# DLRM tower with a compressed interaction network: the first layer's sums over d made by ScalarE's evictions

## The reference

```python
e = stack([tbl_f[ids[:, f]] for f in range(32)], axis=1)      # (2048, 32, 16): b, m, d
x0 = xk = e
outs = []
for W in (W0, W1, W2):                                        # (m, h, k), k = 64; h = 32, 64, 64
    xk = relu(einsum('bmd,bhd,mhk->bkd', x0, xk, W))
    outs.append(sum(xk, axis=2))                              # over d
z = concatenate(outs, axis=1)                                 # (2048, 192)
h = concatenate([z, dense_ctx], axis=1)
h = maximum(h @ W_top1 + b_top1, 0)                           # 512
h = maximum(h @ W_top2 + b_top2, 0)                           # 256
y = h @ W_top3
```

## Time and profile before

| | |
|---|---|
| median of 3 runs | 1216.67 us (1216.64 to 1218.73) |
| the profiled execution's own time | 1227.56 us |
| its span in the profile | 1225.8 us |
| TensorE (PE) matmul busy | 1122.7 us, 92% |
| VectorE (DVE) busy | 1116.5 us, 91% |
| ScalarE (ACT) busy | 731.8 us, 60% |
| GpSimd (POOL) busy | 923.2 us, 75% |
| mean granted clock of TensorE | 0.986 of full speed |

### The profile page before, as it was taken

The page is one execution under the profiler, slowest core; times in us unless marked ns, Lnnn a source line. Parts: engine busy times, 40 slices in busy tenths (PEclk is TensorE's granted clock), DMA queues, the critical chain, the costliest instruction groups (busy, mean ns, idle before and its releaser), DMA issues.

```text
span 1225.8 us, 14619 instructions
## 1 busy us (share of the span) xinstructions
PE 1122.7 (92%) x5312; PEld 395.7 (32%) x5312; DVE 1116.5 (91%) x519; ACT 731.8 (60%) x1361; POOL 923.2 (75%) x642
## 2 busy tenths in 40 slices
PE   0267999999999999999999999999999999999997
PEld 0022233333343333334333333333333333333334
DVE  0158999999999999999999999999999999999994
ACT  0036656765675666666666766576576657657652
POOL 6767888788887878788787878878787887875400
PEclk9878999999999999999999999999999999999998
DMA  5967877657688676768877566787767677776200
GB/s 117 188 126 157 166 152 148 140 120 150 133 167 166 137 147 125 146 128 159 167 149 148 119 144 131 151 165 152 152 130 141 130 146 158 164 153 131 53 1 1
DMA packets 76088, 167.25 MB, mean 136 GB/s; under 512 B 21648, under 2 KB 38944, under 8 KB 76016
## 3 DMA queue, kind: packets, MB, share of 16 engines
q1 hardware_dynamic: 59088, 161.95, 63.1%
q0 software_dynamic: 16384, 4.23, 3.7%
q10 hardware_dynamic: 544, 0.14, 0.1%
HBM read 157.86 MB, written 8.40 MB: 136 GB/s over the span
## 4 chain that ended last, share of the span: by engine, by line
PE 78%; DVE 11%; issue 8%; ACT 2%; another core or an unknown queue 1%; ACTq 0%; DVEq 0%
PE acc L578 72%; DVE p_dve L504 11%; PE acc L648 3%; PE acc L636 1%; PE acc L638 1%; ACT xb L305 1%; PE acc L656 1%; DVE z L531 1%; ACT x_s L314 0%; ACT xa L296 0%; ACT L323 0%; ACT out_l L389 0%; ACT h L418 0%; ACT p_l L323 0%
## 5 line engine op out<-in xcount | busy, mean ns | idle before, releaser
L578 PE MATMUL acc<-p_dve,w_s 128*64 128x512 f32 x3840 | 864.0, 597 | 51.9 <-DVE p_dve L504 48.8
L244 POOL DMA_INDIRECT x_rows<-in_table,ids_s x512 | 488.8, 955 | 145.9 <-issue 132.7
L504 DVE TENSOR_TENSOR p_dve<-spread,xb 128x3072 f32<-128x3072 f32 (+2 forms) x224 | 567.2, 2586 | 16.4 <-PE acc L578 16.4
L504 DVE TENSOR_TENSOR p_dve<-spread,xa 128x2048 f32<-128x2048 f32 (+1 forms) x192 | 495.6, 2637 | 35.2 <-issue 31.1
L578 PEld LDWEIGHTS acc<-p_dve,w_s 128*64 128x64 f32 x3840 | 267.5, 137 | 602.9 <-issue 493.2
L305 ACT ACTIVATE xb<-acc 32x512 f32<-32x512 f32 x512 | 288.8, 564 | 84.5 <-DVE p_dve L504 78.1
L256 POOL TENSOR_TENSOR p_l<-spread,q_tile 128x2048 f32<-128x2048 f32 x62 | 281.8, 4570 | 11.5 <-DMA q_tile<-x_of_steps 8.3
L296 ACT ACTIVATE xa<-acc 64x512 f32<-64x512 f32 x256 | 145.9, 570 | 205.2 <-PE acc L578 110.7
L267 POOL TENSOR_TENSOR p_pool<-spread,x_s 128x1024 f32<-128x1024 f32 x64 | 152.4, 2381 | 121.9 <-PE acc L578 66.3
L578 PE MATMUL acc<-p_l,w_s 128*64 128x512 f32 (+1 forms) x640 | 150.4, 606 | 45.4 <-issue 45.4
L314 ACT ACTIVATE x_s<-acc 64x512 f32<-64x512 f32 x256 | 151.2, 591 | 3.5
(11 more groups left out here) (18 smaller groups left out, 159.1 us busy)
## 6 DMA issues: line engine op xcount, KB each, us to landing
spread<-x_of_steps SPq DMA_DIRECT2D x256, 512.0 KB
q_tile<-x_of_steps SPq DMA_DIRECT2D x128, 128.0 KB
x_rows<-in_table,ids_s POOLq DMA_INDIRECT x512
x_of_steps<-x_rows SPq DMA_DIRECT2D x64, 128.0 KB
w_s<-in_w SPq DMA_DIRECT2D x2, 512.0 KB
wt<-in_w_top SPq DMA_DIRECT2D x1, 512.0 KB
z_all<-in_dense_t ACTq DMA_DIRECT2D x16, 8.0 KB
wt<-in_w_top SPq DMA_DIRECT2D x1, 256.0 KB
```

What stands on the lines that cost most here:

```text
L244: nc.gpsimd.indirect_dma_start(out=x_rows[:, s % 2, i * DIM:(i + 1) * DIM], out_offset=None, in_=table, in_offset=bass.IndirectOffsetOnAxi ...
L504: nc.vector.tensor_tensor(p_dve[:, to:to + n, :], spread[:, s % 3, tile:tile + n, :], over(x[:], n), ALU.mult).then_inc(dve_made, n)
L578: last = nc.tensor.matmul(acc[b * K:(b + 1) * K, :], w, prod[:, b * BLK:(b + 1) * BLK], start=start, stop=stop)
```

## The change

`out_0` and VectorE's `sums(s, 0)` go. In their place ScalarE has `sums_0(s)`: 32 activations (Relu) of 16 columns each, from `acc0` to `out_l`, each of which also returns the sum of its 16 results (`accum_out`) straight into `z`. They stand behind `out_2(s - 2)`, where `out_0` stood behind `x1_s`, in front of `x1_b`. `acc0` is free when `z_made[0]` says so. The MLP's first product moves from behind chunk 5 to behind chunk 8.

```diff
@@ -50,7 +50,7 @@
 GATHERED_BEFORE, THEN = 44, 4
 
 
-MLP1_AFTER, MLP2_AFTER, MLP3_AFTER = 5, 13, 1
+MLP1_AFTER, MLP2_AFTER, MLP3_AFTER = 8, 13, 1
 LATE_MLP1_AFTER, LATE_MLP2_AFTER, LATE_MLP3_AFTER = 10, 14, 3
 
 
...
@@ -338,11 +338,18 @@
                     act.wait_ge(pool_made, pool_from(s - 1, 1) + 1)
                 relu_s(acc0, 1, x1s_ready)
 
-            def out_0(s):
+            def sums_0(s):
+
 
                 if s > 0:
                     act.wait_ge(z_made[0], s)
-                nc.scalar.activation(out_l[:, 0, :], acc0[:], ACT.Relu).then_inc(out_ready[0], 1)
+                if s % 2 == 0 and s >= 4:
+                    act.wait_ge(z_moved, s // 2 - 1)
+                for i in range(SB // 2):
+                    cols = slice(i * DIM, (i + 1) * DIM)
+                    last = nc.scalar.activation(out_l[:, 0, cols], acc0[:, cols], ACT.Relu,
+                                                accum_out=z[:, s // 2 % 2, 0, s % 2, i:i + 1])
+                last.then_inc(z_made[0], 1)
 
             def x1_b(s):
 
...
@@ -443,12 +450,12 @@
             squares(0)
             x1_a(0)
             x1_s(0)
-            out_0(0)
             for s in range(STEPS):
                 t = s // 2 - 2 if s % 2 == 0 and s >= 4 else None
                 x1_b(s)
                 if s >= 2:
                     out_2(s - 2)
+                sums_0(s)
                 if s >= 1:
                     x2_a(s - 1)
                 if s + 1 < STEPS:
...
@@ -471,7 +478,6 @@
                 if s + 1 < STEPS:
                     x1_a(s + 1)
                     x1_s(s + 1)
-                    out_0(s + 1)
             x2_a(STEPS - 1)
             mlp1(TILES - 2)
             x2_b(STEPS - 1)
...
@@ -552,7 +558,6 @@
             for s in range(STEPS):
                 for c, n in GROUPS_L1:
                     if c == NT:
-                        sums(s, 0)
                         if s >= 2:
                             sums(s - 2, 1)
                     layer1(s, c, n)
...
@@ -587,7 +592,7 @@
                     rows = P if c < CP else FIELDS
                     if c == 0 and s > 0:
                         pe.wait_ge(x1b_ready, s)
-                        pe.wait_ge(out_ready[0], s)
+                        pe.wait_ge(z_made[0], s)
                     if c < CP:
                         pe.wait_ge(l0_made, CP * s + c + 1)
                     else:
...
@@ -628,7 +633,7 @@
                 pe.wait_ge(z_moved, t + 1)
                 pe.wait_ge(dense_loaded, 16 * (t + 1))
                 pe.wait_ge(x1b_ready, min(2 * t + 5, STEPS))
-                pe.wait_ge(out_ready[0], min(2 * t + 5, STEPS))
+                pe.wait_ge(z_made[0], min(2 * t + 5, STEPS))
                 if t > 0:
                     pe.wait_ge(mlp_done, 3 * t)
                 for n in range(H1 // P):
```

More of the change, by code:

```diff
@@ L148, in build_kernel @@
         x2b_ready = sem("x2b_ready")
-        out_ready = [sem(f"out{n}_ready") for n in range(3)]
+        out_ready = [sem(f"out{n}_ready") for n in (1, 2)]
         z_made = [sem(f"z{n}_made") for n in range(3)]
@@ L381, in out_1 @@
                     act.wait_ge(z_made[1], s)
-                nc.scalar.activation(out_l[:, 1, :], acc1[s % 2][:], ACT.Relu).then_inc(out_ready[1], 1)
+                nc.scalar.activation(out_l[:, 1, :], acc1[s % 2][:], ACT.Relu).then_inc(out_ready[0], 1)
             def out_2(s):
@@ L388, in out_2 @@
                     act.wait_ge(z_made[2], s)
-                nc.scalar.activation(out_l[:, 2, :], acc2[:], ACT.Relu).then_inc(out_ready[2], 1)
+                nc.scalar.activation(out_l[:, 2, :], acc2[:], ACT.Relu).then_inc(out_ready[1], 1)
             def move_sums(t, to, k, n):
@@ L529, in sums @@
                     dve.wait_ge(z_moved, s // 2 - 1)
-                dve.wait_ge(out_ready[n], s + 1)
+                dve.wait_ge(out_ready[n - 1], s + 1)
                 nc.vector.reduce_sum(z[:, s // 2 % 2, n, s % 2, :],
@@ L600, in layer1 @@
                 if c == 0 and s >= 2:
-                    pe.wait_ge(out_ready[1], s - 1)
+                    pe.wait_ge(out_ready[0], s - 1)
                 if c != POOL_CHUNK:
@@ L614, in layer2 @@
                 if c == 0 and s > 0:
-                    pe.wait_ge(out_ready[2], s)
+                    pe.wait_ge(out_ready[1], s)
                 if c != POOL_CHUNK:
```

## The result

| | before | after |
|---|---|---|
| median, runs side by side | 1217.17 us (1216.64 to 1218.73, 4 runs) | 1206.74 us (1205.21 to 1209.06, 4 runs) |
| ratio, 95% interval | | 0.9914 [0.9894, 0.9934] |
| the same beside the last experiments | 1216.43 us (11 runs) | 1205.72 us (6 runs), 0.9923 [0.991, 0.9937] |
| profiled execution, its span | 1227.56, 1225.8 us | 1205.21, 1203.4 us |

A forecast was written before the change was run, and what follows sets the result against it. The prediction took the chain of waits as the bound, TensorE in the MLP step and VectorE in the other. Gains of 8.3 and 2.4 us, together 10.6, off the 1216.7 us median gave 1206.1 us, range 1203 to 1242.

The forecast's parts named there:

- The reduce that goes: VectorE's reduce in the step without MLP, ahead of products TensorE waits for: 0.59 us in each of 14 pairs, 8.3 us.
- The four early reduces: Before 187 us VectorE runs without waiting for TensorE; four reduces in its way give 4 x 0.59 = 2.4 us.
- The reduce in the MLP step: It lies in the TensorE part of a pair; without it VectorE only waits longer, nothing gained.
- Moving the MLP contraction later costs TensorE nothing: MLP's first contraction in TensorE's MLP step, moved two chunks of four records back: cost 0, as TensorE runs through.
- 32 evictions at 162 ns: ScalarE's new burst behind layer 3's eviction: 5.2 us, the middle of 107 and 216 ns each, under both rooms, cost 0.
- The estimate from the Trainium skill: ScalarE's burst by the skill's figures: 200 ns each, 6.4 us, 0.2 over the first room, gain 8 us instead of 10.6.
- The rooms: Time for ScalarE's burst before delay: 6.2 us before MLP's first contraction, 7.9 us before VectorE needs x-a without MLP.
- Flat: Rival: evictions take 213 to 223 ns, TensorE's wait for the sums eats the gain; about 1216 us, chance 0.10.
- slower: Rival: returned sums drain ScalarE's pipe, 223 to 260 ns each, holding MLP's contraction, then x-a; 1242 us, chance 0.20.
- The much slower one: Rival: ScalarE's evictions do not overlap at all, 347 ns each, 11.1 us a burst; 1329 us, chance 0.12.

The follow-up runs named there:

- the last experiments: The change with VectorE's two remaining sums moved behind layer 2's second group, run again, 1196.33 us; the change itself beside it, 1205.72 us.
- The run that was to show it worth nothing: Against the kernel before: ScalarE makes the first layer's sums only in MLP steps, MLP's first contraction behind chunk 8; 1215.71 us, ratio 0.9993.
- the order alone: The kernel before with all three VectorE sums of a step moved behind the second group of layer 2; 1195.56 us, ratio 0.9826.
- the run with the pauses: The change with VectorE's two remaining sums also moved behind the second group of layer 2; 1374.19 us, and 1196.33 us on another chip.

## Why the prediction was right, and where only by luck

- **The reduce that goes, 0.59 x 14 = 8.3 us.** Right: pairs 70.28 us, 0.60 less. That TensorE's wait would fall from 1.23 to 0.65 us was wrong in its place: it fell to 1.01, and a second wait of 0.36 us, hidden in a merged row, went away.
- **The four early reduces, 2.4 us.** Three of them count, 1.8 us by the two timelines. The first is followed by 10.71 us in which VectorE stands still anyway; the prediction looked for waits for TensorE alone there.
- **The reduce in the MLP step is worth nothing.** In the kernel before, by its trace, yes; wrong in the change, where it gives 0.48 us a pair and pays for the moved contraction. The run that was to show it worth nothing (ratio 0.9993) shows its gain and the move's price cancelling.
- **"Moving the MLP contraction later costs TensorE nothing, as it runs through anyway."** This step failed. Alone the move costs 0.47 us a pair, 6.6 us, because the contraction had been the time in which VectorE got ahead with chunk 8. This error and the one before it cancel, so the sum came out right by luck in this part. The prediction said that VectorE runs ahead of TensorE in an MLP step, but never laid VectorE's group for chunk 8 against TensorE's arrival there.
- **32 evictions at 162 ns, 5.2 us.** 156 ns and 5.04 us. The size held, though 162 was only the middle between two guesses; the rows show two instructions, started 63 and 93 ns apart. The estimate from the Trainium skill (ScalarE: Activation LUTs, What ACT_TABLE_LOAD costs) had 200 ns and 6.4 us; the trace is faster. The statement of its page VectorE: DVE Perf Modes (Two Vector instructions with no wait between them), that an operation which writes out its accumulator is two instructions, holds on ScalarE here as well: 1024 of each.
- **The rooms, 6.2 us before the MLP's contraction and 7.9 before x-a.** 5.2 us of sums would have left 1.0 and 2.7 us; by the runs with more evictions 0.5 and 2.4 were left. With 16 more, TensorE waits 2.04 us behind the first room and VectorE 0.13 behind the second; with 32 more VectorE waits 2.64. What a wait costs was missing: behind a wait of 2.04 us TensorE's clock fell in some pairs, 1.6 us more in a pair that has it.
- **The rivals.** Flat and slower needed 213 ns and more per eviction, and on the chips of the comparison nothing like it was seen. The much slower one was given 0.12 by a lack of overlap; the one place where its size was met had pauses instead.
- The chain of waits names ScalarE's burst for 6% of the span. It follows x-a back into the burst, but x-a was done at 589.43 us and VectorE took it at 592.05 without having waited; a shorter burst would give nothing.

## What to carry to other kernels

Price an instruction by which engine binds in its own stretch, and once more in the stretch that the rest of the change makes: here a reduce that TensorE waited for nowhere was worth half a microsecond a pair once the contraction had moved. When a change has several parts, take each out alone and add the prices up; a run that holds two parts can show nothing only because they cancel. Before work is handed to another engine, try to move it to where its own engine has slack; the order alone gave twice the gain (1195.56 us) and keeps ScalarE out of it. Two rows with the same count and different lengths hide a wait, so compare lengths before trusting the brackets.

## What the runs showed of the hardware that was not expected

- ScalarE's eviction with a returned sum is two instructions, started 63 and 93 ns apart for 128x16 out of PSUM, and their reported lengths grow from 0.17 to 0.44 us within a burst at a constant pitch.
- On one chip, bursts of 64 small ScalarE instructions ran with pauses, 10.1 to 11.0 us in place of 5.0, and the kernel took 1374 us where it took 1196 on another. The Trainium skill (Perfetto Trace Analysis, Optimizing Scalar/DVE Operations) advises grouping into larger operations when an engine is saturated; ScalarE was not saturated here (66% busy in the run with the pauses). The 29 bursts with pauses are those in which GpSimd issues gathers, but no run of this study shows what makes ScalarE pause.
- After a wait of 2.04 us TensorE's granted clock fell in some pairs (0.66 over the next 5 us) and stayed at 1.00 in others; after 4.95 us the next window stood at 0.50.
